# The first stage turned round: the next chunk's maxima and exponentials ahead of both norms

## The reference

```
k, v = k_in @ Wk, v_in @ Wv;  r = sigmoid(r_in @ Wr)
step: max_out = maximum(mx, ck + tf); e1 = exp(mx - max_out); e2 = exp(ck + tf - max_out)
      out = (e1 * num + e2 * cv) / (e1 * den + e2)
      max_st = maximum(mx + td, ck); e1s = exp(mx + td - max_st); e2s = exp(ck - max_st)
      num, den, mx = e1s * num + e2s * cv, e1s * den + e2s, max_st
x = layernorm(x + r * rwkv @ Wo)
x = layernorm(x + fp8_linear(x))
x, z = split(x @ W_in); x = silu(causal_conv(x, taps) + b)   # then the long convolution, * silu(z), @ W_out
```

## Time and profile before

| | |
|---|---|
| Median of three runs | 470.0 us (469.54 to 470.42) |
| The profiled execution | 471.45 us, of which the span of its instructions is 469.6 us |
| First stage | to about 138.5 us |
| TensorE busy, whole span | 422.7 us (90%) |
| VectorE busy | 329.7 us (70%) |
| ScalarE busy | 191.6 us (41%) |
| GpSimd busy | 20.9 us (4%) |

### The profile page before, as it was taken

One profiled execution on the slowest core, in us unless ns is written; L12 is line 12 of the kernel. 1 busy time (PEld: TensorE's weight loads), 2 busy tenths in 40 slices (PEclk: granted clock), 3 DMA queues, 4 the chain that ended last, 5 costly groups with the idle time before them and its releaser, 6 DMA issues.

```text
span 469.6 us, 4230 instructions
## 1 busy us (share of the span) xinstructions
PE 422.7 (90%) x1422; PEld 209.5 (45%) x1422; DVE 329.7 (70%) x675; ACT 191.6 (41%) x314; POOL 20.9 (4%) x36
## 2 busy tenths in 40 slices
PE   4872997989979989999999999999999998999893
PEld 1331464755845355444544444433734433343361
DVE  4999898799862994497988777391753862274385
ACT  1342658543125521435234455253037525324341
POOL 0010202111000000000000000000000000000001
PEclk9996999989999999999999999999999999999996
DMA  6300000040000000000000000000000000000001
GB/s 220 142 1 0 1 1 0 2 145 0 1 2 2 0 0 0 1 1 0 1 1 0 1 0 22 1 1 0 0 0 1 23 1 0 1 0 1 0 0 45
DMA packets 5152, 7.27 MB, mean 15 GB/s; under 512 B 1080, under 2 KB 4236, under 8 KB 4876
## 3 DMA queue, kind: packets, MB, share of 16 engines
q1 hardware_dynamic: 3972, 4.80, 3.0%
q10 hardware_dynamic: 1160, 2.21, 1.3%
HBM read 5.95 MB, written 1.05 MB: 15 GB/s over the span
## 4 chain that ended last, share of the span: by engine, by line
PE 55%; DVE 9%; ACT 5%; issue 2%; POOL 0%; POOLq 0%; DVEq 0%
PE ring L1216 21%; PE ring L1194 7%; PE ring L1211 4%; PE ring L1196 4%; PE specbank L253 3%; PE ring L1224 3%; PE timebank L265 2%; PE ring L1238 2%; PE ring L1242 1%; PE ring L1239 1%; DVE hm L1409 1%; ACT L1348 1%; PE ring L1207 1%; PE ring L1231 1%; PE ring L1235 1%
## 5 line engine op out<-in xcount | busy, mean ns | idle before, releaser
L1216 PE MATMUL ring<-hm,wc 128*128 128x512 f32 (+1 forms) x252 | 108.6, 580 | 0.0
L1216 PEld LDWEIGHTS ring<-hm,wc 128*128 128x128 f32 x252 | 46.1, 190 | 61.0 <-issue 52.8
L1409 DVE SCALAR_TENSOR_TENSOR hm<-xtm,cst,h 128x512 f32<-128x512 bf16 x48 | 33.3, 746 | 7.9 <-ACT h L1322 7.9
L197 PE MATMUL bankA<-wconv,h2w 128*128 128x256 f32 x128 | 34.0, 412 | 5.1 <-ACT h2w L568 5.1
L1336 ACT ACTIVATE gts<-ring 128x512 f32<-128x512 f32 (+1 forms) x18 | 9.9, 550 | 52.7 <-PE ring L1216 52.7
L1322 ACT ACTIVATE h<-ring,vec 128x512 f32<-128x512 f32 x32 | 21.9, 687 | 18.1 <-PE ring L1196 15.7
L197 PEld LDWEIGHTS bankA<-wconv,h2w 128*128 128x128 f32 x128 | 24.9, 204 | 9.5 <-ACT h2w L568 5.8
L1497 DVE SCALAR_TENSOR_TENSOR f2e<-hl,f2e 128x512 f32<-128x512 f32 (+1 forms) x9 | 5.7, 629 | 26.7 <-ACT hl L1365 26.7
L1211 PE MATMUL ring<-hm,wc 64*128 64x512 f32 (+1 forms) x84 | 22.9, 621 | 0.4 <-DVE hm L1409 0.4
L1333 ACT ACT_TABLE_LOAD x8 | 10.3, 1283 | 28.4 <-PE ring L1216 28.4
L265 PE MATMUL timebank<-cst,abc 128*128 128x256 f32 x96 | 21.5, 380 | 0.0
(11 more groups left out here) (265 smaller groups left out, 751.9 us busy)
## 6 DMA issues: line engine op xcount, KB each, us to landing
wc<-in_w_c SPq DMA_DIRECT2D x1, 1664.0 KB, 6.9
cst<-in_const ACTq DMA_DIRECT2D x1, 1096.0 KB
out<-xall SPq DMA_DIRECT2D x8, 128.0 KB, 1.9
wc<-in_x_feat SPq DMA_DIRECT2D x1, 768.0 KB, 12.3
bconv<-in_bcast SPq DMA_DIRECT2D x1, 512.0 KB, 6.8
wc<-in_k_time ACTq DMA_DIRECT2D x1, 512.0 KB
wc<-in_x_feat ACTq DMA_DIRECT2D x1, 256.0 KB, 3.6
wa<-in_w_a SPq DMA_DIRECT2D x1, 256.0 KB, 3.5
```

The lines of the kernel that those rows point to most:

```text
L197: pe.matmul(at, h2w[:, n, h * P + tap:h * P + tap + P], wconv[:, tap, :], start=(tap == 0), stop=False)
L1216: ins = pe.matmul(dst[:, at], wc[:, w:w + P], hm[:, seat(j, made + g - 1), at], start=False, stop=(g == PAIRS - 1))
L1409: dve.scalar_tensor_tensor(hm[:, seat(j, k), :], picked, cst[:, C_EG + g:C_EG + g + 1], h[:, g, :], ALU.is_equal, ALU.mult).then_inc(S["hm ...
```

## The change

The four engines' `one(c)` are written in another order. No instruction's size or arithmetic is changed.

- VectorE: `maxima` runs for chunk c+1 and stands behind `output_end(c)`, ahead of `residual_end(c-1)` and `residual_mid(c)`. maxima(0) and the preparation of layer two's weights stand ahead of the turns.
- ScalarE: a turn begins with norm two of chunk c-2 and norm one of chunk c-1 in a row, then piece 3 of chunk c-3 (from the turn before), the window, the input of `rounded`, the key of chunk c+1, piece 0, the values of chunk c+1, `y1b`, the exponentials of chunk c+1, and pieces 1 and 2. Piece 3 stays in its turn only in turns 4 and 5.
- TensorE: the key projection of chunk c+1 begins the turn, the value projection stands between `turn2` and `turn1`, the receptance projection behind piece 0, and the output projection of chunk c behind piece 1, in the same turn. Piece 3 of chunk c-3 stands between `turn2` and `turn1` of the next turn. Turn 3 begins with `forward_half(0, 0)`.
- GpSimd: `factors` of norm two of chunk c-1, then of norm one of chunk c, as VectorE now delivers them.

VectorE's part of the diff:

```diff
                 def one(c):
                     if valid(c):
-                        maxima(c)
-                    if c == 0:
-                        linear_weights()
-                    if valid(c - 1):
-                        residual_mid(c - 1)
...
+                    if valid(c + 1):
+                        maxima(c + 1)
...
+                    if valid(c - 1):
                         residual_end(c - 1)
+                    if valid(c):
+                        residual_mid(c)
```

More of the change, by code:

```diff
@@ L593, in _, with keys @@
             def _(pe):
-                def project(c):
+                def keys(c):
                     if valid(c):
@@ L601, in project, with values @@
                         pe.matmul(psk[:, :], wmix[:, 1, 0, :], prev(hT, c), start=False, stop=True).then_inc(k_done, 1)
+                def values(c):
+                    if valid(c):
                         after(pe, kv_copied, c)
[L603 to L605 removed]
@@ new lines, in output @@
+                def output(c):
+                    if valid(c):
+                        if c == 0:
+                            pe.wait_ge(weights_mixed, 7)
+                        pe.wait_ge(rwkv_ready, c + 1)
+                        after(pe, x1_ready, c)
+                        for j in range(TILES):
+                            at = c * WIN + 1 + j % HALVES * P
+                            pe.matmul(pso[:, j * P:(j + 1) * P], hT[:, j // HALVES, at:at + P], ident, start=True, stop=False)
+                            ins = pe.matmul(pso[:, j * P:(j + 1) * P], rwkv[:, j * P:(j + 1) * P], wa[:, W_O:W_O + P], start=False, stop=True)
+                        ins.then_inc(wo_done, 1)
@@ new lines, in spectra @@
+                def spectra(c):
+                    if c == 0:
+                        pe.wait_ge(consts_in, 5 * 16)
+                        pe.wait_ge(taps_ready, 1)
+                    for m in (2 * c, 2 * c + 1):
+                        after(pe, spec_kept, m - 1)
+                        for kh in range(HALVES):
+                            ins = pe.matmul(piecebank[m % 2][:, :].rearrange("p (d c) -> p d c", d=2), cst[:, C_FWD + kh * 2 * WIN + m * P:][:, 0:P],
+                                            kt[:, kh:kh + 3:2, :], start=(kh == 0), stop=(kh == HALVES - 1))
+                        ins.then_inc(spec_done, 1)
@@ L706, in _ @@
                 pe.wait_ge(weights_mixed, 6)
-                project(0)
+                keys(0)
+                values(0)
+                receptance(0)
                 turns(pe, one, ahead=1)
```

131 lines of the change are left out of this document (63 added, 68 removed).

## The result

| | before | changed |
|---|---|---|
| Median | 470.21 us (469.54 to 472.02) | 474.71 us (474.44 to 475.28) |
| Ratio | | 1.0090 [1.0073, 1.0108] |
| Profiled execution, its span | 471.45 us, 469.6 us | 474.93 us, 473.1 us |
| First stage ends (VectorE's last instruction) | 138.2 us | 139.0 us |
| Second stage, from there | 331.4 us | 334.1 us |

The forecast was 469.5 us in a range of 468.2 to 471.9 us, with "same" as likeliest. The ratio is that of the two kernels' times, with its 95% interval in brackets. The changed kernel lies 4.5 us above the kernel before and outside the range. In the traces 3.5 us of span are to be explained: 0.85 in the first stage, 2.65 in the second. Three of the executions behind this document (one of b1, one of b2, one of the kernel before) took 632 to 1491 us and are left out of the ratios.

A forecast was written before the change was run, and what follows sets the result against it. The prediction took TensorE's row from chunk 2's first half piece to `project_block` as the first stage's bound. Window +1.55, `turn1(3)` -0.5, full clock -1.67 and releases +0.1 gave -0.5 us: 470.0 to 469.5 us, range 468.2 to 471.9.

The forecast's parts named there:

- What ends the first stage: End of first stage: chunk 2's first half piece starts, then TensorE's row to `project_block`, then 8.1 us on VectorE.
- VectorE's lead is worth nothing: Behind the start of chunk 2's first half piece (96.93 us), VectorE being ahead doesn't shorten the first stage.
- The swap's gain on VectorE: VectorE, turns 2 and 3: reordering removes waits, gaining 1.35 us by turn 2 and up to 2.5 us by turn 3.
- ScalarE in turn 2: Exponentials ahead of keeping pieces 1 and 2 take 7.5 us in all, uncovered, delaying `forward_half(0, 0)` to about 74.0 us.
- TensorE in turn 3, VectorE's wait for `y1b`: Turn 3: pieces come later, `lin(2)` at 87.8 us; VectorE waits 2.3 us ahead of `residual_end(2)`, losing its 2.4 us lead.
- S: Start of `forward_half(0, 0)` in turn 3, forecast between 74.0 and 75.0 us and taken as 74.6 us.
- The window in turn 4: ScalarE, turn 4: norm one ahead of the window starts chunk 2's pieces at 98.5 us, 1.55 us later than 96.93.
- I take full clock, 1.67 us less: TensorE, turn 4: chunk 2's first half piece, slow before, was assumed to run at full clock, saving 1.67 us.
- rival B: One more slow-clock stretch on TensorE, ahead of `forward_half(0, 0)` or in turn 4: 1.6 us back, 471.1 us; chance 0.27.
- The second stage ... stay: Second stage, the 8.1 us behind `project_block` and the weight transfer into `wc` were taken as unchanged.
- C: TensorE's row isn't the bound, VectorE keeps 2.4 us; needs `lin(2)` 2 us earlier; 467.6 us; chance 0.12.
- D: ScalarE's queue delays the window in turns 3 and 4, outweighing the gain if `forward_half(0, 0)` starts beyond 76.0; 472.0 us; chance 0.14.

The follow-up runs named there:

- b1: Changed kernel with ScalarE's window ahead of norm one and the kept gate piece, and TensorE's first half piece ahead of `turn1`; 473.79 us, ratio 1.0059.
- b2: b1 with two unused matmuls at the begin of TensorE's turn 4 and two behind its last first-stage piece; 471.50 us, ratio 1.0013.
- c1: b2 with more unused TensorE matmuls, five in turn 2 and two ahead of `forward_half(0, 0)`; 468.56 us, ratio 0.9958.
- c3: Kernel before with unused matmuls in TensorE's gaps of turns 1, 3 and 4 and behind its last first-stage piece; 470.17 us, ratio 0.9985.
- a4: Kernel before with VectorE's `maxima(c+1)` ahead of `residual_end(c-1)` and ScalarE's exponentials ahead of norm two, TensorE's order kept; 472.30 us, ratio 1.0031.
- b3: Changed kernel with two unused matmuls at the begin of TensorE's turn 4 and two behind its last first-stage piece; 470.39 us, ratio 0.9985.
- c2: b3 with more unused TensorE matmuls, five in turn 2 and two ahead of `forward_half(0, 0)`; 469.99 us, ratio 0.9977.
- a1: Changed kernel with two unused matmuls on TensorE behind its last first-stage piece, ahead of the barrier; 471.88 us, ratio 1.0027.
- a2: Kernel before with one unused matmul (0.86 us) on TensorE ahead of `project_block(0)`; 473.34 us, ratio 1.0054.
- c4: Changed kernel with two unused matmuls at the begin of TensorE's turn 4 alone; 473.00 us, ratio 1.0036.
- a3: Changed kernel with ScalarE's window ahead of norm one and of keeping gate piece 3 in turns 2 to 4; 474.60 us, ratio 1.0073.

## Why the prediction was wrong, point by point

- **What ends the first stage: right for both kernels.** TensorE's row from chunk 2's pieces to `project_block`. The changed trace shows it, with VectorE idle for 4.16 us ahead of `residual(0)`, and c1, where 2.84 us at chunk 2's half piece are 2.83 us at `residual(0)`. "VectorE's lead is worth nothing" behind that start is too strong: in c3 and a4, the old order on TensorE with that row at full clock, TensorE waits for VectorE there.
- **The swap's gain on VectorE: right.** Scans(3) came without a wait, at 72.68 (73.25 with the 0.57 us of the early start) where 74.0 was forecast; the waits of rows 2 are gone, but for 0.5 us.
- **ScalarE in turn 2: right, somewhat too long.** `forward_half(0, 0)` was forecast for 74.0 to 75.0, and 74.6; 73.34 in the trace, 73.9 with the 0.57 us of its early start. The slow stretch of turn 2, half of which the forecast let through to this point, doesn't show there. The three exponentials and the loads between 67.48 and 72.60 are those of the sum. The load took 1.28 us and the instruction behind it came at 68.77, 0.01 us later. The Trainium skill, "ScalarE: Activation LUTs", section "What ACT_TABLE_LOAD costs", adds a drain of 1.38 us to a switch of tables; it isn't there in this trace either.
- **TensorE in turn 3, VectorE's wait for `y1b`: right as a mechanism, 1.3 us late as a whole.** From `forward_half(0, 0)` to chunk 1's half piece it was S + 6.9 by the forecast and 6.82 in the trace. But S came 1.26 us earlier than forecast, and `lin(2)` with it (86.56 for 87.8). VectorE waited 1.97 us for 2.3 forecast, and part of its lead survived, where the forecast had all of it gone.
- **The window in turn 4: right in place and size, and the stamp is partly luck.** The half piece was forecast for 98.5 and started at 98.36, but by two errors that cancel: the transposes came 1.1 us earlier than the 95.1 of the forecast, and the lower clock took 1 us from there on. At full clock the step that the window is in, from transposes to half piece, took 3.36 us in b3 and 3.37 in c2, for 3.4 forecast and 2.01 in the kernel before (94.92 to 96.93). c1 against c2 measures the place of window and half piece together at 1.7 us.
- **"I take full clock, 1.67 us less": wrong.** This term of the sum should have been about zero. It was rival B, given 0.27. The gate piece between the gaps (1.71 us instead of 1.02), `turn1` and the half piece (3.46 us) were slow. It cost 2.45 us between the transposes and `forward_half(0, 1)` in the traces, 2.0 us by the ratios of b3 and a1. That TensorE had more work between the gaps was no protection.
- **"The second stage ... stay": wrong, and the larger part.** No rival had it. The prediction had read that a 2.38 us gap pulls the clock down and had looked for gaps in the reordered turns alone. The gap of 2.63 us at the barrier, followed by 0.76 us more, is of the same kind, and in the kernel before the clock stood it; the prediction doesn't speak of this gap at all. The lower clock behind it is worth 2.65 us in the traces and 2.9 us in a1.
- **The sum.** -0.5 us was forecast for the first stage; it came at +0.85. The slow stretch of turn 4 adds 2.45 and the transposes, 1.1 us earlier than forecast, take that off again (0.57 of it is the trace's early start). With the 2.65 us behind the barrier that is the span's +3.5. The medians differ by 4.5 us because the traced run of the kernel before lay 1.24 us above its median and that of the changed kernel 0.22 above.
- **The rivals C and D** did not come about: `lin(2)` came 1.3 us earlier than before and not the 2 us that C needs, TensorE's row still ended the stage, and `forward_half` wasn't beyond 76.

What stays open: why the clock fell behind the barrier in the changed kernel and, by the times, seldom in the kernel before. Only one of the changed kernel's four runs is traced, but all four lie at 474.4 to 475.3 us; of the kernel before 4 of 85 lie there (474.66 to 474.88), and 81 below 472.2. a2 shows that the old order has it too when it ends 0.9 us later; c4's trace and median show that the new order can still have it when it ends 1.1 us earlier. The Trainium skill, "TensorE: Matmul & The Clock Gate", section "What's actually happening", says that the monitor of the gate runs by itself and isn't reset by a kernel. It agrees that like gaps had unlike outcomes here, and that a2 and c4 spread over 2.5 and 3.6 us, against 0.8 and 0.95 in c1 and c2; c3, with its gaps filled too, spread over 2.6. That only the timing relative to the monitor decides is argued, not shown.

## What to carry to other kernels

When TensorE ends a stage, an idle gap of 2 us or somewhat more is not worth its own length alone, but may cost as much again behind it (up to 2.65 us here, and nothing in other runs); count every such gap of the whole program, also of stages that the change only shifts, and put a price and a chance on each. A kernel with such gaps can lose more by a small delay than the delay itself (a2: 0.54% for 0.9 us, which is 0.2%), so two orders should be compared with the gaps filled in both: here the changed order went from 1.009 to 0.998 by that and the old one to 0.9985, and only then the place of the window (1.7 us) could be seen. Before moving a step ahead of a wait, look at what the partner engine has queued behind its own next wait: the window moved alone brought nothing that could be told (a3), and with the half piece it brought 1.7 us (c1 against c2); the half piece alone wasn't run.

## What the runs showed of the hardware

- The same 2.6 us gap, with the same 30 us of dense work ahead, left the clock at 1.00 in one kernel and brought it to 0.50, the lower level, in the other (138.68 and 139.55 us). With the gap cut to 0.92 us it stayed up (a1).
- Shorter gaps behave alike: 0.94 and 1.36 us of idle time, with 0.66 us of work between, ended at the lower clock in the kernel before (the row at 96.93, 3.66 us) and at full clock in a4 (the row at 97.56, 1.99 us).
- With four gaps filled the changed orders' runs spread over 0.8 and 0.95 us (c1, c2), where the changed kernel with one gap filled spread over 3.6 us (c4). The old order with its gaps filled still spread over 2.6 us (c3).
- A filling can move the slow stretch instead of removing it: in c3 one came behind a 2.10 us wait that the filled kernel had in another turn.
